# An edge sort, a softmax over edges and an aggregation, re-ordered: norms before the first digit count, three-part transposes, rounded two-part denominators

## What is computed

```python
h = jnp.maximum(_layernorm(x), 0.0)                   # then a second layer norm with gain and bias
xl, xr = h @ Wl, h @ Wr
e = einsum('ehc,hc->eh', leaky_relu(xl[src] + xr[dst], 0.2), att)
ex = exp(e - segment_max(e, dst)[dst])
denom = segment_sum(ex, dst)
out = segment_sum(ex / (denom[dst] + 1e-16) * xl[src], dst) + gat_bias
x = x + out                                           # then norm and MLP
```

## Time and profile before

| | us |
|---|---|
| median of three runs (1311.36 to 1313.65) | 1313.23 |
| the profiled execution | 1309.4 |
| its span, first to last instruction | 1307.3 |
| PE busy (share of the span) | 1118.4 (86%) |
| DVE busy | 1056.8 (81%) |
| ACT busy | 704.7 (54%) |
| POOL busy | 446.5 (34%) |
| mean granted TensorE clock, of 1 | 0.922 |

### The profile page before, as it was taken

One profiled execution on the slowest core, in us unless ns is written; L12 is line 12 of the kernel. 1 busy time (PEld: TensorE's weight loads), 2 busy tenths in 40 slices (PEclk: granted clock), 3 DMA queues, 4 the chain that ended last, 5 costly groups with the idle time before them and its releaser, 6 DMA issues.

```text
span 1307.3 us, 16447 instructions
## 1 busy us (share of the span) xinstructions
PE 1118.4 (86%) x5143; PEld 822.0 (63%) x5165; DVE 1056.8 (81%) x1607; ACT 704.7 (54%) x1346; POOL 446.5 (34%) x411
## 2 busy tenths in 40 slices
PE   0899778867777761899999997799999979999998
PEld 0479546655565551455555553698888867788886
DVE  9898799799999998999999999757677564664634
ACT  1720120077777761588888886676555666343430
POOL 5630530177777771566666660000012000000000
PEclk9999898888777775899999999799999989999999
DMA  4000000177777781566666663100001010100002
GB/s 173 19 23 9 9 25 1 27 205 213 214 215 214 213 204 33 156 187 183 187 187 183 187 177 117 48 1 25 1 33 47 1 57 1 33 1 1 1 1 80
DMA packets 40921, 120.55 MB, mean 92 GB/s; under 512 B 6572, under 2 KB 6878, under 8 KB 40836
## 3 DMA queue, kind: packets, MB, share of 16 engines
q0 software_dynamic: 28160, 93.74, 25.8%
q1 hardware_dynamic: 12676, 25.74, 5.5%
HBM read 114.23 MB, written 5.22 MB: 91 GB/s over the span
## 4 chain that ended last, share of the span: by engine, by line
PE 65%; DVE 23%; ACT 6%; issue 2%; POOL 2%; DMA 1%; ACTq 0%; SPq 0%; DVEq 0%
PE bank L808 10%; PE bank L699 10%; PE bank L752 8%; PE bank L738 8%; PE bank L597 8%; PE bank L711 7%; PE bank L786 6%; DVE arena L1391 5%; DVE arena L1393 5%; PE bank L581 3%; POOL arena L522 2%; DVE counts L1193 2%; ACT counts L993 2%; PE bank L558 2%; PE bank L702 1%
## 5 line engine op out<-in xcount | busy, mean ns | idle before, releaser
L522 POOL DMA_INDIRECT arena<-left_table,arena x352 | 355.3, 1009 | 237.9 <-DVE arena L1475 91.2
L699 PE MATMUL bank<-arena 128*128 128x512 f32 x352 | 187.2, 619 | 4.3 <-DVE arena L1475 4.3
L648 PE MATMUL bank<-xr_hi,hot_t 128*128 x176 | 99.0, 563 | 61.7 <-ACT bank L963 60.7
L993 ACT ACTIVATE counts<-bank 128x1280 f32 x88 | 108.9, 1237 | 52.1 <-PE bank L711 52.1
L702 PEld LDWEIGHTS bank<-arena 128*128 128x128 f32 x352 | 67.3, 191 | 85.2 <-issue 84.5
L808 PE MATMUL bank<-hw_hi,counts_r 128*128 128x512 f32 (+1 forms) x300 | 119.7, 399 | 1.1 <-DVE arena L1661 1.1
L808 PE MATMUL bank<-hw_lo,counts_r 128*128 128x512 f32 (+1 forms) x300 | 118.1, 394 | 0.0
L963 ACT ACTIVATE bank<-arena 128x1024 f32<-128x1024 f32 x88 | 90.4, 1028 | 45.3 <-DVE arena L1391 40.0
L1391 DVE SCALAR_TENSOR_TENSOR arena<-bank,arena 128x1024 f32<-128x1024 f32 x88 | 107.7, 1224 | 6.9 <-PE bank L648 4.1
L1393 DVE TENSOR_REDUCE arena<-arena 128x16 f32<-128x1024 f32 x88 | 107.4, 1220 | 3.0
L597 PE MATMUL bank<-arena 125*125 125x160 f16 (+1 forms) x640 | 100.1, 331 | 10.8 <-DVE arena L1241 10.8
(11 more groups left out here) (239 smaller groups left out, 2421.4 us busy)
## 6 DMA issues: line engine op xcount, KB each, us to landing
arena<-left_table,arena POOLq DMA_INDIRECT x352, 3.7
arena<-in_L_gnn_W_dram SPq DMA_DIRECT2D x8, 512.0 KB, 5.0
arena<-in_L_gnn_W_dram SPq DMA_DIRECT2D x2, 1536.0 KB, 10.8
arena<-in_L_gnn_W_dram SPq DMA_DIRECT2D x3, 1024.0 KB, 5.2
left_table<-arena SPq DMA_DIRECT2D x10, 260.0 KB, 2.0
arena<-in_x_dram SPq DMA_DIRECT2D x1, 2304.0 KB
arena<-in_x_dram SPq DMA_DIRECT2D x9, 256.0 KB
out_dram<-state SPq DMA_DIRECT2D x9, 256.0 KB
```

The source lines that it names most:

```text
L522: g.indirect_dma_start(out=gathered[n % DEPTH][:, i, :], out_offset=None, in_=left_table, in_offset=bass.IndirectOffsetOnAxis(ap=src_of[:, ...
L648: ins_ = t.matmul(bank[:, 2 * (n % ZRING) + i, :], mine, part[:, bass.ds(at, 1), :].rearrange("p b n -> p (b n)"), start=False, stop=(part ...
L699: t.matmul(bank[:, s0, :], hot[c % 4], w[:, i, :], start=(i == 0), stop=(i == 1))
L993: a.activation(counts[:, :, bass.ds(at * P, P)], flat[:, COUNT_AT:COUNT_AT + NP].rearrange("p (b n) -> p b n", n=P), ACT.Copy).then_inc(*c ...
```

## The change

- x is loaded in ten loads with a semaphore for every two blocks; the last two blocks follow W left.
- VectorE does most of both norms and the whole of `wa` (products too) before the low count, and the rest behind it. The attention columns are one set of 16-column products for both sides. ScalarE takes one square root of eps at its start. POOL's bias adds and splits wait for the comparison in `count_digits` (`matched`): blocks 0 to 3 for the low one, the others for the high one.
- 24 projection steps precede the low base numbers, 24 follow, none lie within the permutation, 18 follow it, 24 come last.
- The reduce in `place_edges` becomes a tree of adds; for the high digit, base and mask are one instruction for each digit.
- Softmax: the last add of scores is part of the layout, in three parts, which TensorE transposes one by one; the scans read PSUM; the larger of both ways is taken in two halves before the carried ends are known; subtraction, Exp, transposes back and copies go in three parts. ScalarE clears the sums.
- Denominators: the weights are split into a rounded and a remaining part (`den_parts`, 18 columns with two of ones), and `hot` is rounded, so one record replaces two. Message sums and denominators are added in one instruction from a ring of two. Low one-hots are made for four columns at once.
- MLP: another order of VectorE's first steps, a second `turned_f` for block 1.

PARTS is (0, 4), (4, 8), (8, 11); DEN is 18. The diff, cut (a line of "..." marks what is left out):

```diff
-NORM_STEPS = [2, 4, 6, 6, 6]
...
+NORM_STEPS = [6, 18, 3, 3, 0]
+COUNT_STEPS, LOW_STEPS, HIGH_STEPS = 24, 24, 18
+PLACE_STEPS = STEPS - COUNT_STEPS - LOW_STEPS - HIGH_STEPS
...
-    s.dma_start(x_in[:, 0:NB - 1, :], ins["x"][0:(NB - 1) * P, :].rearrange("(b p) d -> p b d", p=P)).then_inc(d_x, 16)
...
+    def load_x(t):
+        for b in range(t * TWO, (t + 1) * TWO):
...
+            s.dma_start(x_in[0:rows_in(b), b, :], ins["x"][b * P:b * P + rows_in(b), :]).then_inc(d_x[t], 16)
+    for t in range(NG2 - 1):
+        load_x(t)
...
+    load_x(NG2 - 1)
...
-    for p, w in zip(products, (w_left, w_right)):
-        g.tensor_tensor(p.rearrange("p (k n) -> p k n", n=D), w, over(att_linear, 1, KC), ALU.mult).then_inc(*att_weighted.up())
...
-        g.tensor_tensor(state[:, b, :], state[:, b, :], gat_bias, ALU.add).then_inc(*biased.up())
...
+    def add_bias(first, end):
+        for b in range(first, end):
...
+            g.tensor_tensor(state[:, b, :], state[:, b, :], gat_bias, ALU.add).then_inc(*biased.up())
+    for nth, (bias_end, split_end) in enumerate(((2 * TWO, SPLIT_FIRST), (NB, NB))):
+        g.wait_ge(matched.sem, nth + 1)
+        add_bias(biased.value, bias_end)
+        while right_split.value < split_end:
...
-                    ins_ = t.matmul(bank[:, 4 + side, 0:HEADS], trans[b % 3][:, k, :], wa[:, side, k, :], start=(k == 0), stop=(k == KC - 1))
...
+            for k in range(KC):
+                ins_ = t.matmul(bank[:, 4 + b % 2, 0:2 * HEADS], trans[b % 3][:, k, :], wa[:, k, :, :].rearrange("p i h -> p (i h)"), start=(k == 0), stop=(k == KC - 1))
...
+    advance(projecting, COUNT_STEPS)
...
-    advance(projecting, sum(NORM_STEPS) + LOW_STEPS)
-    pick(0, EP, EJ, lambda j: beside(projecting, COLUMN_STEPS, j))
+    advance(projecting, LOW_STEPS)
+    pick(0, EP, EJ)
...
+    for k0, k1 in PARTS:
+        t.wait_ge(scores_laid.sem, k1)
+        for k in range(k0, k1):
+            ins_ = t.transpose(flat[:, k * P:(k + 1) * P], score_rows[:, k, :], ident[:, :])
...
-        ins_ = t.transpose(flat[:, k * P:(k + 1) * P], turned[:, k * P:(k + 1) * P], ident[:, :])
...
+    for k0, k1 in PARTS:
+        t.wait_ge(shifted_down.sem, SK)
+        t.wait_ge(exp_ready.sem, k1)
+        for k in range(k0, k1):
+            ins_ = t.transpose(flat[:, k * P:(k + 1) * P], turned[:, k * P:(k + 1) * P], ident[:, :])
...
+            t.wait_ge(den_lo_ready.sem, 1)
...
-            t.wait_ge(sums_added.sem, n - SUMS + 1)
+            t.wait_ge(sums_added.sem, n - 1)
...
-            t.matmul(bank[:, s0, :], hot[c % 4], w[:, i, :], start=(i == 0), stop=(i == 1))
...
-            t.matmul(bank[:, SUMS + n % 2, 0:HEADS + 1], hot[c % 4], weights[:, c, :], start=(i == 0), stop=(i == 1)).then_inc(*tile_summed.up())
+            t.matmul(bank[:, psum, :], as_float(hot[c % 4]), w[:, i, :], start=(i == 0), stop=(i == 1))
+            t.matmul(bank[:, psum + 1, 0:DEN], hot[c % 4], den_parts[:, c, :], start=(i == 0), stop=(i == 1)).then_inc(*tile_summed.up())
...
+                ins_ = t.matmul(flat[:, COUNT_AT + at:COUNT_AT + end], low_hot[n // 2 % 2][:, :, c % QUARTET], code_hot[c % 4][:, at:end],
...
+    a.wait_ge(eps_ready.sem, 1)
+    a.activation(deviation[:, 0, :], eps[:, :], ACT.Sqrt).then_inc(*ao.up())
...
+    a.wait_ge(scores_laid.sem, SK)
+    a.activation(sums, over(zero[:, :].broadcast_to([P, NB]), 2, D + DEN), ACT.Copy).then_inc(*agg_zero.up())
...
+    a.activation(den_parts[:, :, 2 * HEADS:DEN], over(ones[:, 0:1].broadcast_to([P, NC]), 2, 2), ACT.Copy).then_inc(*den_ones.up())
+    hot_of(0)
+    hot_of(1)
+    for k0, k1 in PARTS:
+        a.wait_ge(shifted_down.sem, k1)
+        a.activation(turned[:, k0 * P:k1 * P], turned[:, k0 * P:k1 * P], ACT.Exp).then_inc(*exp_ready.up(k1 - k0))
+    a.wait_ge(weights_ready.sem, SK)
+    a.activation(den_parts[:, :, 0:HEADS], weights, ACT.Copy).then_inc(*den_hi_ready.up())
...
+        move_turned(turned_f_of(b), 6 + b % 2, ("L0_gnn_ln2_g", 0), ("L0_gnn_ln2_b", 0)).then_inc(*rows_moved.up())
...
-        v.tensor_tensor(by_digit(match, radix), over(digit[R0, :], 1, radix), digits[R0, 0:radix, :], ALU.is_equal).then_inc(*vo.up())
...
+        v.tensor_tensor(by_digit(match, radix), over(digit[R0, :], 1, radix), digits[R0, 0:radix, :], ALU.is_equal).then_inc(*matched.up())
+        v.wait_ge(*matched.now())
...
-        v.tensor_tensor(r3, by_digit(running, radix), over(base_of[R0, 0:radix], 2, EJ), ALU.add).then_inc(*vo.up())
...
-        v.tensor_tensor(r3, r3, by_digit(match, radix), ALU.mult).then_inc(*vo.up())
...
-        v.tensor_reduce(place[R0, :], r3.rearrange("p k j -> p j k"), AX.X, ALU.add).then_inc(*vo.up())
+        if radix == HIGH:
+            for k in range(radix):
+                ins_ = v.scalar_tensor_tensor(r3[:, k, :], by_digit(running, radix)[:, k, :], base_of[R0, k:k + 1], by_digit(match, radix)[:, k, :], ALU.add, ALU.mult)
+            ins_.then_inc(*vo.up())
+        else:
+            v.tensor_tensor(r3, by_digit(running, radix), over(base_of[R0, 0:radix], 2, EJ), ALU.add).then_inc(*vo.up())
...
+            v.tensor_tensor(r3, r3, by_digit(match, radix), ALU.mult).then_inc(*vo.up())
+        n = radix
+        while n > 1:
+            half = n // 2
...
+            out_ap = r3[:, 0:half, :] if n > 2 else place[R0, :].unsqueeze(1)
+            v.tensor_tensor(out_ap, r3[:, 0:half, :], r3[:, n - half:n, :], ALU.add).then_inc(*vo.up())
+            n -= half
...
+    def fold_weights(side, w):
...
+        p = products[side]
+        v.tensor_tensor(p.rearrange("p (k n) -> p k n", n=D), w, over(att_linear, 1, KC), ALU.mult).then_inc(*att_weighted.up())
...
+        v.tensor_reduce(wa[:, :, side, :], p.rearrange("p (k h c) -> p k h c", k=KC, c=C), AX.X, ALU.add).then_inc(*att_folded.up())
...
+    norm_x(0, 4)
...
+    fold_weights(0, w_left)
+    fold_weights(1, w_right)
+    norm_x(4, 5)
...
-    before_projections()
+    norm_x(5, NG2 + 3)
...
+    v.tensor_copy(low_iota, over(iota_node[:, 0:P], 2, QUARTET)).then_inc(*vo.up())
...
-    for part in range(2):
...
-        v.tensor_tensor(score, score, target_linear[:, :, part, :], ALU.add).then_inc(*vo.up())
...
-    v.tensor_copy(score_rows.rearrange("p k (g h) -> p k g h", h=HEADS), score.rearrange("p (g k) h -> p k g h", k=SK)).then_inc(*scores_laid.up())
+    v.tensor_tensor(score, score, target_linear[:, :, 0, :], ALU.add).then_inc(*vo.up())
...
+    by_run = lambda ap: ap.rearrange("p (g k) h -> p k g h", k=SK)
+    for k0, k1 in PARTS:
+        v.tensor_tensor(score_rows[:, k0:k1, :].rearrange("p k (g h) -> p k g h", h=HEADS), by_run(score)[:, k0:k1], by_run(target_linear[:, :, 1, :])[:, k0:k1],
+                        ALU.add).then_inc(*scores_laid.up(k1 - k0))
+    scores = flat[:, 0:RUN]
...
-    v.tensor_copy(turned, flat[:, 0:RUN]).then_inc(*vo.up())
+    v.tensor_tensor_scan(ahead_max, reset, scores, FAR, ALU.add, ALU.max).then_inc(*vo.up())
...
+    def both_ways(first, end):
+        v.tensor_tensor(ahead_max[:, first:end], ahead_max[:, first:end], behind_max[:, first:end], ALU.max).then_inc(*vo.up())
+    v.wait_ge(*ends_laid.now())
+    both_ways(0, RUN // 2)
...
+    both_ways(RUN // 2, RUN)
...
-    v.scalar_tensor_tensor(ahead_max, not_first, carry[:, 0:1], ahead_max, ALU.add, ALU.max).then_inc(*vo.up())
-    v.scalar_tensor_tensor(behind_max, not_last, carry[:, 1:2], behind_max, ALU.add, ALU.max).then_inc(*vo.up())
...
-    v.tensor_tensor(ahead_max, ahead_max, behind_max, ALU.max).then_inc(*vo.up())
...
-    v.tensor_tensor(turned, turned, ahead_max, ALU.subtract).then_inc(*shifted_down.up())
...
-    v.tensor_copy(weights[:, :, 0:HEADS].rearrange("p (g k) h -> p k g h", k=SK),
-                  flat[:, 0:RUN].rearrange("p (k g h) -> p k g h", g=SG, h=HEADS)).then_inc(*weights_ready.up())
+    for only, n in ((not_first, 0), (not_last, 1)):
+        v.scalar_tensor_tensor(ahead_max, only, carry[:, n:n + 1], ahead_max, ALU.add, ALU.max).then_inc(*vo.up())
...
+    for k0, k1 in PARTS:
+        v.tensor_tensor(turned[:, k0 * P:k1 * P], scores[:, k0 * P:k1 * P], ahead_max[:, k0 * P:k1 * P], ALU.subtract).then_inc(*shifted_down.up(k1 - k0))
+    for k0, k1 in PARTS:
+        v.wait_ge(exp_turned.sem, k1)
+        v.tensor_copy(by_run(weights)[:, k0:k1], flat[:, k0 * P:k1 * P].rearrange("p (k g h) -> p k g h", g=SG, h=HEADS)).then_inc(*weights_ready.up(k1 - k0))
...
-        v.tensor_tensor(d, d, bank[:, s0, :], ALU.add)
...
-        v.tensor_tensor(d, d, bank[:, SUMS + n % 2, 0:HEADS + 1], ALU.add).then_inc(*sums_added.up())
...
+        v.tensor_tensor(d, d, flat[:, psum:psum + D + DEN], ALU.add).then_inc(*sums_added.up())
...
+        if n == 0:
+            v.wait_ge(den_hi_ready.sem, 1)
+            v.tensor_tensor(den_parts[:, :, HEADS:2 * HEADS], weights, as_float(den_parts[:, :, 0:HEADS]), ALU.subtract).then_inc(*den_lo_ready.up())
+        if n % 2 == 0:
+            if n >= 4:
+                v.wait_ge(pair_counted.sem, n - 2)
```

(35 more changed lines are left out.)

210 lines of the change are left out of this document (97 added, 113 removed).

## The result

| | before | after |
|---|---|---|
| median, us | 1313.0 (4 runs) | 1275.97 (4 runs, 1274.2 to 1276.84) |
| the profiled execution, us | 1309.4 | 1274.2 |
| its span, us | 1307.3 | 1272.5 |
| mean granted TensorE clock | 0.922 | 0.921 |

The account below looks back on a forecast made before the run. VectorE was taken to carry the edge sort, a serial chain the softmax, TensorE the pair steps, VectorE and ScalarE the MLP start. Gains 12.7 + 4.4 + 6.8 + 10.6 + 5.2 = 39.7 us gave 1273, range 1256 to 1290.

Parts of the forecast that it names:

- First statistics, norms, folds: Start of the edge sort: norms start near 5.7 us, folded products take 2.3 each, ranking starts 4.3 us earlier.
- POOL's price: Edge sort: POOL's moved adds and splits hold VectorE, 60% of 9 and of 11 at 1.0: 5.4 and 6.6 us.
- Rival (a): Edge sort: POOL's adds hide, 51.7 us gained in all, 1261 us; chance 0.20.
- Rival (b): Edge sort: each of 20 POOL instructions takes its full 1.25 us from VectorE, 25 instead of 12: 1286 us; chance 0.12.
- The forty instructions: High digit of the edge sort: base and mask as 40 instructions at 0.23 us, 9.2 us instead of 13.7.
- The tree: High digit of the edge sort: a tree of adds takes 7.6 us instead of the reduce's 11.2.
- The pace of the permutation: First permutation of the edge sort: VectorE sets the pace, 4.78 us a batch, 47.7 us instead of 55.4.
- Softmax: Softmax over scores: weights ready 8.7 us earlier, 1.9 lost before the first product, net gain 6.8 us, ends 4 and 9.
- Pair step: Aggregation's 88 pair steps: one record per denominator saves 0.06 us twice, 3.16 to 3.04 a pair, 10.6 us in all.
- Rival (c): Aggregation: the pair step stays at 3.16 us because the rounded weight load is exposed, 1284 us; chance 0.12.
- Rival (e): Pair loop: TensorE, no longer full, loses its clock; slower, up to 1540 us for all 88 pairs; chance 0.03.
- (d): Start of the edge sort: blocks of x land together near 10 us, 4.3 us less gain, 1278 us; chance 0.03.

Follow-up runs that it names:

- e12: Changed kernel with POOL's bias adds moved to the ends of both permutations, five each, and splits waiting for the digit counts: median 1265.35 us, ratio to before 0.9641.
- e7: Changed kernel with the high digit's tree of adds made one reduce again, the forty instructions kept: 1276.5 us.
- e2: Changed kernel with a dummy Exp on ScalarE before its wait for the shifted scores: ramp copy to first message product 29.76 us against 30.69.
- e9: Changed kernel with ScalarE reading the block number for the copy of counts between its two target one-hots: pair step 2.974 us against 2.987.
- e4: Changed kernel with the denominators as float32 products again, two records instead of one: pair step 3.161 us against 2.987.
- e6: Changed kernel with VectorE's low-digit count ahead of the norms again: 1283.0 us.
- e8: Changed kernel with two bias adds after the low comparison, five after the first permutation's first hot batch, three after the high comparison: 1276.5 us.

## Why the prediction was right, and where it was off

- **First statistics, norms, folds.** Forecast 5.7, came at 5.67; the folded products took 2.3 each as worked out. First product forecast "near 79": 79.37.
- **POOL's price** ("I take 60% of 9 and of 11 at 1.0"). The forecast held 60% of 20 instructions at 1.0, 12 us in all. The price of a single meeting was right (1.06). The share was the mis-sized factor. e12 measures the ten adds at 8.5 us, where the forecast allowed them 6. The ten splits come to about 6.7, an estimate from the changed kernel's held rows: 3.7 in the low phase (0.95 in L1249, 2.0 in the tree of L1255, 0.7 in an instruction on two words) and 3.0 in the high one (1.0 in the forty, 2.0 in the tree). Together some 15 instead of 12. Rival (a), hidden adds, is out. Rival (b) has the mechanism right and the sum too high. The Trainium skill (SBUF — State Buffer, "SBUF: two separate sides") states it as an exclusive lock on a shared port pair, in which the side that comes second waits for the whole instruction. The traces agree: an add waits through a whole scan, and a VectorE pass beside a queued add takes 1.06 longer. But not every instruction meets VectorE: in e12 the split at 44.54 ran beside statistics that still took 1.28 for two, and e7's reduce was not held.
- **The forty instructions.** "I take 0.23": 0.298 alone. 9.2 became 11.9, 2.7 us, the largest miss in the price of one form; the 12.94 of the profile holds one split besides. The form still beats two passes, by 1.7 and not by 4.5.
- **The tree.** "7.6 of adds": 9.6, of which 2.0 is held by two splits. Its own price was right.
- **The pace of the permutation.** 4.78 forecast, 4.90 came. The term took VectorE for the one that sets the pace. The products of a batch take 4.8 themselves, and in every second batch TensorE waits 0.19 for VectorE and VectorE 0.24 for TensorE. That the rings of two buffers make them take turns is my reading, not tested. From the first product to the permutation's end it took 48.7 us instead of 47.7. The gain at that end was 10.9, forecast 12.7.
- Together the sort gave 10.2 instead of 17.1 (about 3.2 for POOL, 2.7 for the forty, 1.0 for the pace), and the second permutation came at 190, not 183; it stayed under the 195 beyond which the sum would have been wrong. The first message product came 15 us earlier, not 24.
- **Softmax**: 5.6 for 6.8. The step that failed is one I left out: the load of Exp's table, 1.28 us, which the kernel before had in idle time and which now stands behind the wait for the shifted scores. e2 gave 0.93 of the 1.2 back by an Exp ahead of that wait.
- **Pair step**: "0.06 less, twice", in truth 0.11 less each (0.12 before, 0.01 in e9), less 0.03 that the counts' six products then took longer. 14.7 instead of 10.6. That the record is what gives was right (e4). That ScalarE "works 2.7 and stays under" was not: with its waits between instructions it comes to 2.99 from copy to copy, and it and TensorE's 2.97 end the step within 0.02 of each other. Rival (c) is out. Rival (e) too: 0.99 granted in the loop before and after. So is (d), as the loads came when they should.
- **MLP start**: 5.2 forecast, 5.4 came.

The errors had both signs: 6.9 and 1.2 too much, 4.1 too little. That the total came within 3 us of 1273 is in part luck, their sum. What they leave, 0.9 in the scores and 0.2 behind the MLP's start, I have not looked into.

## What to carry to other kernels

In this kernel an elementwise add on POOL (1.25 us alone) cost VectorE 0.85 to 1.1 us whenever it got in between elementwise work of VectorE, small copies and casts too; statistics and reduces ran beside it unslowed. So don't ask when POOL is free, ask when VectorE waits for someone else; the end of a stretch in which TensorE finishes a chain is such a place (e12). A scan or another long pass belongs where the next engine's results are late (e6), not where it happens to be ready. Look in the trace where a function table is loaded and where the wait ahead of its first use stands. Carried by the using instruction, the wait came after the load (488.55 and 518.53 before); as an instruction of its own, it held the load as well (503.22 after). A dummy use ahead of the wait took the load off the path (e2). And when the busiest engine has been relieved, redo the sum for the others with their waits between instructions in it, not only their work.

## What was not expected of the hardware

- Adds queued behind VectorE's passes slip in between them, one by one: one-hot passes of 1.19 us in a row took 2.25 each (e8). But not always: in e12 a split whose row starts at 155.27, among the forty instructions (151.04 to 162.97), was done only at 164.10, 8.83 us later. In the changed kernel one that started at 160.39, among the same forty, was done in 1.45. Why the one got in and the other did not is not shown.
- A product of 18 columns on two rounded inputs adds 0.01 us to TensorE's chain between products of 512 columns (e9); as float32 0.13 (e4).
- The scores stage moves the same gathers at 211 GB/s in the changed kernel's profile and at 168 in that of e2, on another chip; the stage took some 58 us more with the same instructions. What slowed them isn't shown.
